# A state-space and spectral network on one core: the first layer's 68 slots written out, in place of a loop over pairs of them

## The chip, the cores and the metric

The kernel runs on one core of a Trainium2 chip. Its engines are PE (TensorE, matmuls, with its weight loads shown as PEld), DVE (VectorE), ACT (ScalarE), POOL (GpSimd) and SP (SyncE), which here only issues DMA transfers. Each runs its own instruction stream, and they wait for each other with semaphores. The metric is the device time of one execution, in microseconds.

## What is computed

The input is a batch of 4 images of 128 channels and 128 x 128 points, in float32. Two layers follow each other; the change is in the first. That one cuts each image into windows of 8 x 8 points and treats the 64 points of a window as a sequence:

```python
tn = (t - mu) * jax.lax.rsqrt(var + 1e-05) * ln_g + ln_b
xz = tn @ W_in + b_in                      # 256 inputs xi, 256 gates z
xc = sum((xp[:, k:k + L, :] * conv_w[:, k] for k in range(K))) + conv_b
xc = jax.nn.silu(xc)
dbl = xc @ W_x                             # rank 8 for delta, 16 rows of B, 16 of C
delta = jax.nn.softplus(dr @ dt_w + dt_b)
def step(h, inputs):
    dA = jnp.exp(d_t[:, :, None] * A)
    h = dA * h + (d_t * x_t)[:, :, None] * B_t[:, None, :]
    y = jnp.einsum('nds,ns->nd', h, C_t)
y = (ys.transpose(1, 0, 2) + xc * D) * jax.nn.silu(z)
out = y @ W_out + b_out                    # and + x
```

The second layer normalises over channels, filters in the frequency domain with 16 complex filters mixed by `Theta`, and ends in a two-matmul MLP with gelu.

## The kernel before

The program has four parts, each a block of five instruction streams: `setup`, `layer0` (the first layer), `spectral` and `mlp` (the second). The first layer works on 64 blocks of 1,024 tokens: a block is 8 rows of one image, 16 windows. It is done in halves of 512 tokens, for 16 states each, so a block has 32 **steps**; a step is one state of one half. In a step DVE scans (L919, `state`), PE or POOL makes what drives the scan (PE transposes `drive_r` at L591 from ACT's `ub`; POOL multiplies `drive_d` at L1034 from a row of B that SP has loaded as `b_all`), ACT makes the decay (L734), DVE or POOL multiplies the state with C (L930 with a row that PE spread into a PSUM bank at L582, L1045 with `c_all` loaded by SP), and PE adds the product into `y_acc` (L604). Between the steps lie the other jobs of the layer: mean and variance, the matmuls of `xz` and the convolution (L641, L646), `rows` and `c_rows` (L754, L755 on ACT, L945 on DVE), delta, the gate, the output and the first transform of the next layer.

The work is pipelined over blocks in **slots**. In slot m the 32 steps are those of block m; at fixed places among them stand the jobs that prepare blocks m + 1 and m + 2 and finish blocks m - 1 and m - 2. The order on every engine is written out by hand, in tables (`JOBS`, `AT`) that give each job its half step. With 64 blocks there are 68 slots, m = -2 to 65; in the first and last four some of the work is missing. Buffers alternate with the parity of m.

`slots` calls each engine's `body` for the slots in order. It writes out the first four, runs the 60 slots m = 2 to 61 as a loop of 30 passes, an even and an odd slot in each, and writes out the last four. In the loop the slot's number depends on the register `j`, and so does the value of every wait: `need` then waits for a value that register arithmetic (L182 as the recorded line) has computed. The loop is a construct of each engine's own stream: at its end stand an addition, a compare and a branch back (L167). DVE also computes, once a slot, the means and variances of eight rows in eight short instructions at L980; this document uses them as a clock mark of a slot.

Of the kernel before, what the change touches and what calls it, by code (L numbers as in the profile page):

```python
# [158 lines left out]

def slots(eng, body, blocks):  # L160
    rounds = (0, 0)
    for m in range(-2, 2):
        slot = Slot(m, True, m >= -1, m >= 0, m >= 1, False, rounds)
        body(slot, m % 2)
        rounds = tuple(r + k for r, k in zip(rounds, slot.size))
    per = tuple(sum(j[3] == bank for j in JOBS) for bank in range(2))
    with eng.Fori(0, (blocks - 4) // 2) as j:  # L167
        for i in range(2):
            body(Slot(j * 2 + 2 + i, True, True, True, True, True,
                      tuple(j * (2 * k) + (r + k * i) for r, k in zip(rounds, per))), i)  # L170
    rounds = tuple(r + k * (blocks - 4) for r, k in zip(rounds, per))
    for m in range(blocks - 2, blocks + 2):
        slot = Slot(m, False, m < blocks - 1, m < blocks, m <= blocks, True, rounds)
        body(slot, m % 2)
        rounds = tuple(r + k for r, k in zip(rounds, slot.size))

# [237 lines left out]
def layer0(nc, a, wt, rows_dram, x1_dram, y_dram, blocks):  # L414
    with ExitStack() as ctx:
# [87 lines left out]
        def _(sp):  # L503
# [65 lines left out]
            sp.sem_inc(s["x1_stored"], 16)  # L569
            sp.sem_inc(s["yo_stored"], 16)  # L570
            slots(sp, body, blocks)
            sp.wait_ge(s["x1_stored"], 16 * blocks + 16)
            sp.wait_ge(s["yo_stored"], 16 * blocks + 16)

        @block.tensor
        def _(pe):
# [129 lines left out]
            def body(S, p):  # L706
                for n in range(NSTEP):
# [9 lines left out]
                    jobs(S, p, 2 * n + 1)  # L717

            slots(pe, body, blocks)

        @block.scalar
        def _(act):
# [179 lines left out]

            act.preload_act_table_set(TABLES)
            slots(act, body, blocks)

        @block.vector
# [718 lines left out]
```

## Time and profile before

| | |
|---|---|
| median of 3 runs | 9539.61 us (9535.7 to 9547.48) |
| the profiled execution | 9544.83 us |
| its span, first to last instruction | 9543.0 us |
| mean granted TensorE clock | 0.986 |
| instructions recorded | 181,899 |
| PE, POOL, DVE, ACT busy, share of the span | 91%, 84%, 87%, 81% |
| DMA packets of the two queues that carry program code | 391 and 357 |

The span is what the trace covers, 1.8 us less than the execution's time. The first layer fills it from the beginning to about 6840 us, the spectral part to about 8990, the MLP the rest. A granted clock of 1 is TensorE at 2.4 GHz, of 0.5 at 1.2 GHz. An idle time put down to "issue" is one in which the engine waited for nothing that the trace shows.

### The profile page before, as it was taken

What the parts mean: (1) busy time and instruction counts of PE and PEld (TensorE: products, weight loads), DVE (VectorE), ACT (ScalarE), POOL (GpSimd) and SP (SyncE); (2) the same over time, 40 slices, a digit from 0 to 9 for tenths busy, and PEclk for the clock granted to TensorE, in tenths of its full rate; (3) what the DMA queues carried; (4) which work ended last, traced back from release to release, by engine and by line L of the source; (5) the groups of instructions that cost most, each with busy time, mean ns of one, the idle gap of its engine ahead of it and who ended that gap; (6) DMA issues with size and microseconds to landing.
All of it is one profiled execution on the core that took longest, in us unless ns stands there. A gap on an engine that the chain in (4) does not pass through costs nothing. (4 is left out here: it accounts for less than half of the span.)

```text
span 9543.0 us, 181899 instructions
## 1 busy us (share of the span) xinstructions
PE 8679.4 (91%) x54525; PEld 6752.8 (71%) x54525; DVE 8330.0 (87%) x8144; ACT 7711.4 (81%) x13926; POOL 8059.3 (84%) x3865
## 2 busy tenths in 40 slices
PE   7998999999899999989999999999799999999899
PEld 4666666666666666666666666666688888888788
DVE  5998999999889999998999999899788888888766
ACT  6998999999899999999999999999555555555577
POOL 5999999999999999999999999999688888888500
PEclk9999999999999999999999999999899999999999
DMA  3333333333333333333333333333200100010255
GB/s 90 113 115 113 109 117 109 113 110 119 109 108 114 115 114 108 117 112 110 110 119 113 110 116 109 114 108 120 76 32 31 36 31 32 31 36 31 78 185 178
DMA packets 648652, 933.96 MB, mean 98 GB/s; under 512 B 79961, under 2 KB 277601, under 8 KB 643553
## 3 DMA queue, kind: packets, MB, share of 16 engines
q1 hardware_dynamic: 647904, 924.64, 31.0%
q8 instruction: 391, 6.41, 0.3%
q14 instruction: 357, 2.92, 0.1%
HBM read 778.38 MB, written 146.04 MB: 97 GB/s over the span
## 5 line engine op out<-in xcount | busy, mean ns | idle before, releaser
L1045 POOL TENSOR_TENSOR prod<-state,c_all 128x1024 f32<-128x1024 f32 x1280 | 3028.2, 2370 | 176.8 <-DVE state L919 167.9
L919 DVE TENSOR_TENSOR_SCAN state<-decay_d,drive_d 128x1024 f32<-128x1024 f32 x1024 | 2337.2, 2282 | 158.0 <-issue 86.0
L1034 POOL TENSOR_TENSOR drive_d<-du,b_all 128x1024 f32<-128x1024 f32 x1024 | 2422.9, 2366 | 53.0 <-DMA b_all<-bc_rows 48.9
L919 DVE TENSOR_TENSOR_SCAN state<-decay_r,drive_r 128x1024 f32<-128x1024 f32 x1024 | 2325.0, 2271 | 28.4 <-PE drive_r L591 26.1
L604 PEld LDWEIGHTS y_acc<-ident,prod 128*128 128x128 f32 x16384 | 1861.5, 141 | 627.8 <-issue 532.5
L604 PE MATMUL y_acc<-ident,prod 128*128 128x128 f32 x16384 | 2152.3, 275 | 40.6 <-POOL prod L1045 36.8
L1342 DVE SCALAR_TENSOR_TENSOR sum_d<-bank_d,filt,sum_d 128x512 f32<-128x512 f32 x2470 | 1679.6, 744 | 268.2 <-PE bank_d L1250 241.3
L1389 POOL TENSOR_TENSOR sum_p<-sum_p,scaled 128x1024 f32<-128x1024 f32 x650 | 1551.7, 2387 | 261.5 <-ACT scaled L1300 229.5
L747 ACT ACTIVATE ub<-ut,bt 128x256 f32<-128x256 f32 x4096 | 1739.0, 499 | 16.1 <-PE drive_r L591 16.1
L1300 ACT ACTIVATE scaled<-bank_p,filt 128x512 f32<-128x512 f32 x1560 | 944.1, 688 | 734.5 <-PE bank_p L1250 660.0
L734 ACT ACTIVATE decay_d<-delta,neg_a 128x504 f32<-128x504 f32 x2048 | 1312.0, 674 | 64.0 <-DVE state L919 63.2
L734 ACT ACTIVATE decay_r<-delta,neg_a 128x504 f32<-128x504 f32 x2048 | 1344.0, 706 | 0.0
L591 PE MATMUL drive_r<-ident,ub 128*128 128x128 f32 x8192 | 1100.4, 278 | 234.6 <-issue 115.1
L591 PEld LDWEIGHTS drive_r<-ident,ub 128*128 128x128 f32 x8192 | 945.4, 143 | 456.5 <-issue 402.1
L930 DVE TENSOR_TENSOR prod<-state,job_bank 128x1024 f32<-128x1024 f32 x768 | 925.4, 1205 | 112.9 <-PE job_bank L582 107.1
L641 PE MATMUL job_bank<-x_in,tap_w 128*128 128x512 f32 (+3 forms) x2048 | 966.0, 594 | 3.7 <-DVE c_rows L945 2.4
L1250 PE MATMUL bank_d<-th_high,x_high 128*128 128x256 f32 x2600 | 792.5, 305 | 6.3 <-DVE x_low L1352 2.5
L1250 PE MATMUL bank_d<-th_low,x_high 128*128 128x256 f32 x2600 | 734.9, 283 | 0.0
L1250 PE MATMUL bank_d<-th_high,x_low 128*128 128x256 f32 x2600 | 734.8, 283 | 0.0
L641 PEld LDWEIGHTS job_bank<-x_in,tap_w 128*128 128x128 f32 x2048 | 353.6, 190 | 319.0 <-issue 301.8
L1052 POOL TENSOR_TENSOR delta<-delta,soft 128x512 f32<-128x512 f32 x256 | 326.8, 1277 | 288.6 <-ACT soft L791 288.6
L1250 PE MATMUL bank_p<-th_high,x_high 128*128 128x256 f32 x1560 | 474.2, 304 | 57.1 <-ACT scaled L1300 57.1
(155 smaller groups left out, 14712.8 us busy)
## 6 DMA issues: line engine op xcount, KB each, us to landing
c_all<-bc_rows SPq DMA_DIRECT2D x1280, 256.0 KB, 3.3
b_all<-bc_rows SPq DMA_DIRECT2D x1024, 256.0 KB, 3.8
ys<-row_spectra SPq DMA_DIRECT2D x130, 256.0 KB, 2.8
column_sums<-tt SPq DMA_DIRECT2D x130, 256.0 KB, 2.2
x_in<-in_x_dram SPq DMA_DIRECT2D x64, 512.0 KB, 4.5
x_res<-in_x_dram SPq DMA_DIRECT2D x64, 512.0 KB, 4.6
x_rows<-x SPq DMA_DIRECT2D x64, 512.0 KB, 4.5
row_spectra<-z SPq DMA_DIRECT2D x64, 512.0 KB, 3.7
```

Source lines behind the costliest of these rows:

```text
L591: mm = pe.matmul(drive_r[:, hf, g * P:(g + 1) * P], ub[place_of(RSTEPS, n, NS_UB)][:, g, hf * P:(hf + 1) * P], wt["ident"][:], start=True, ...
L604: mm = pe.matmul(y_acc[:, g, hf * P:(hf + 1) * P], prod[n % NP][:, hf, g * P:(g + 1) * P], wt["ident"][:], start=(n % NS == 0 and hf == 0 ...
L641: mm = pe.matmul(o[:, :, k:WT], wt["tap_w"][:, K - 1 - k, hf * P:(hf + 1) * P], v[:, :, 0:WT - k], start=(k == 0), stop=(k == K - 1), skip ...
L734: last = act.activation(dst[:, hf, :, 1:WT], delta[:, hf, q * HT:(q + 1) * HT].rearrange("p (w t) -> p w t", t=WT)[:, :, 1:WT], ACT.Exp, s ...
L747: last = act.activation(ub[place_of(RSTEPS, n, NS_UB)][:, g, :], ut[q][:, g, :], ACT.Copy, scale=bt[q][:, g, st:st + 1])
L919: dve.tensor_tensor_scan(state[n % NT][:].rearrange("p h t -> p (h t)"), decay[:].rearrange("p h w t -> p (h w t)"), drive[:].rearrange("p ...
L1034: pool.tensor_tensor(drive_d[place_of(DSTEPS, n, ND)][:], du[:, :, q * HT:(q + 1) * HT], b_all[slot][:].unsqueeze(1).to_broadcast([P, 2, HT]),
L1045: pool.tensor_tensor(prod[n % NP][:], state[n % NT][:], c_all[slot][:].unsqueeze(1).to_broadcast([P, 2, HT]), ALU.mult).then_inc(s["prod_g ...
L1250: mm = pe.matmul(o, x[p][:, part, b, :], th[:, 2 * pair:2 * pair + 2, :].rearrange("p l h -> p (l h)"), start=(b % 2 == 0 and i == 0), sto ...
L1300: act.activation(scaled[n % 2][:, i, out, :].rearrange("p (b h) -> p b h", b=B), bank_p[:, :, i, :], ACT.Copy, scale=filt[p][:, kind, 2 * ...
L1342: dve.scalar_tensor_tensor(acc, src, factor, acc, ALU.mult, ALU.add).then_inc(s["summed_d"], 1)
L1389: pool.tensor_tensor(acc, acc, scaled[n % 2][:, i], ALU.add).then_inc(s["summed_p"], 1)
```

## The change

`slots` loses the loop. All 68 slots are written out, with m as a plain number; the flags of what a slot contains follow from m. Every value waited for is then a constant. What each engine computes, in which order, and which semaphores it waits for, stay the same.

```diff
 def slots(eng, body, blocks):
     rounds = (0, 0)
-    for m in range(-2, 2):
-        slot = Slot(m, True, m >= -1, m >= 0, m >= 1, False, rounds)
-        body(slot, m % 2)
-        rounds = tuple(r + k for r, k in zip(rounds, slot.size))
-    per = tuple(sum(j[3] == bank for j in JOBS) for bank in range(2))
-    with eng.Fori(0, (blocks - 4) // 2) as j:
-        for i in range(2):
-            body(Slot(j * 2 + 2 + i, True, True, True, True, True,
-                      tuple(j * (2 * k) + (r + k * i) for r, k in zip(rounds, per))), i)
-    rounds = tuple(r + k * (blocks - 4) for r, k in zip(rounds, per))
-    for m in range(blocks - 2, blocks + 2):
-        slot = Slot(m, False, m < blocks - 1, m < blocks, m <= blocks, True, rounds)
+    for m in range(-2, blocks + 2):
+        slot = Slot(m, m < blocks - 2, -1 <= m < blocks - 1, 0 <= m < blocks, 1 <= m <= blocks, m >= 2, rounds)
         body(slot, m % 2)
         rounds = tuple(r + k for r, k in zip(rounds, slot.size))
```

In the built program the first layer's loop bodies hold 1299 entries on PE (a matmul and its weight load counted once), 611 on ACT, 398 on DVE, 278 on POOL and 188 on SP. Written out, the first layer has 36,604 on PE, 14,649 on ACT, 7,875 on DVE, 5,822 on POOL and 2,948 on SP; before it had 3,585, 1,522, 895, 642 and 378.

The place that matters is where an odd slot ends and an even one begins. On DVE this is, before the change, the end of the loop body: the last steps of the odd slot, register arithmetic between them, and the branch.

```order
L182 REGISTER_ALU
L919 SCALAR_TENSOR_TENSOR state2<-decay_d,drive_d3 128x1024
L182 REGISTER_ALU
L919 SCALAR_TENSOR_TENSOR state3<-decay_r1,drive_r 128x1024
L182 REGISTER_ALU x2
L930 TENSOR_TENSOR prod2<-state2,job_bank0 128x1024
L167 REGISTER_ALU
L167 COMPARE_AND_BRANCH
```

The branch leads back to the start of the body, where the register values of the pass are made and the even slot begins:

```order
L167 ISA
L182 ISA
L919 SCALAR_TENSOR_TENSOR state0<-decay_d,drive_d0 128x1024
L182 ISA
L919 SCALAR_TENSOR_TENSOR state1<-decay_r0,drive_r 128x1024
L182 ISA x2
L945 TENSOR_TENSOR c_rows1<-job_bank1,c_rows1 16x512
```

After the change the same place of DVE's stream, between slot 3 and slot 4 (the line numbers are ten lower, L909 for L919):

```order
L920 TENSOR_TENSOR prod0<-state0,job_bank0 128x1024
L909 SCALAR_TENSOR_TENSOR state2<-decay_d,drive_d3 128x1024
L909 SCALAR_TENSOR_TENSOR state3<-decay_r1,drive_r 128x1024
L920 TENSOR_TENSOR prod2<-state2,job_bank0 128x1024
L909 SCALAR_TENSOR_TENSOR state0<-decay_d,drive_d0 128x1024
L909 SCALAR_TENSOR_TENSOR state1<-decay_r0,drive_r 128x1024
L935 TENSOR_TENSOR c_rows1<-job_bank1,c_rows1 16x512
L920 TENSOR_TENSOR prod0<-state0,job_bank0 128x1024
```

The arithmetic and the branch are gone, and nothing that computes has moved.

## Rows read from the trace of the kernel before

**Rows 1.** The page: busy time of each engine, share of the span, instructions.

```profile
PE 8679.4 (91%) x54525; PEld 6752.8 (71%) x54525; DVE 8330.0 (87%) x8144; ACT 7711.4 (81%) x13926; POOL 8059.3 (84%) x3865
```

**Rows 2.** Table of stretches: us, busy per engine, PEclk, DMA share, GB/s.

```profile
3029.50:3036.00 6.50, 2.47 (x19) 1.92 (x17) 3.92 (x3) 2.83 (x5) 5.16 (x4) 1.00 0.96 262
3036.00:3040.00 4.00, 3.83 (x12) 2.56 (x13) 3.81 (x2) 0.27 (x1) 4.00 (x3) 0.57 0.25 91
3134.50:3236.80 102.30, 94.64 (x586) 69.29 (x585) 95.47 (x75) 96.61 (x180) 96.78 (x49) 1.00 0.37 115
```

**Rows 3.** Timeline of DVE at L980: start us, us, operation.

```profile
381.40 0.63 DVE L980 BATCH_NORM_AGGREGATE mv<-stats 128x2 f32<-128x6 f32 x8
...
484.78 0.63 DVE L980 BATCH_NORM_AGGREGATE mv<-stats 128x2 f32<-128x6 f32 x8
...
3001.69 0.64 DVE L980 BATCH_NORM_AGGREGATE mv<-stats 128x2 f32<-128x6 f32 x8
...
3108.98 0.64 DVE L980 BATCH_NORM_AGGREGATE mv<-stats 128x2 f32<-128x6 f32 x8
...
3211.30 0.64 DVE L980 BATCH_NORM_AGGREGATE mv<-stats 128x2 f32<-128x6 f32 x8
...
6565.12 0.63 DVE L980 BATCH_NORM_AGGREGATE mv<-stats 128x2 f32<-128x6 f32 x8
```

**Rows 4.** Timeline at one turn; in brackets the idle time before, and releaser.

```profile
3031.36 0.61 PE L612 MATMUL y_acc<-diag_d,xc 128*128 128x128 f32 x4
...
3032.23 1.20 DVE L930 TENSOR_TENSOR prod<-state,job_bank 128x1024 f32<-128x1024 f32 x1
...
3035.68 2.35 POOL L1034 TENSOR_TENSOR drive_d<-du,b_all 128x1024 f32<-128x1024 f32 x1 [1.34 <-DMA b_all<-bc_rows]
...
3036.17 1.96 PE L591 MATMUL drive_r<-ident,ub 128*128 128x128 f32 x8 [4.20 <-issue]
3036.19 2.29 DVE L919 TENSOR_TENSOR_SCAN state<-decay_d,drive_d 128x1024 f32<-128x1024 f32 x1 [2.77 <-issue]
...
3039.73 0.69 ACT L770 ACTIVATE zs<-job_bank,z_b 128x512 f32<-128x512 f32 x1 [7.03 <-PE job_bank L646]
...
3043.01 0.68 DVE L945 TENSOR_TENSOR c_rows<-job_bank,c_rows 16x512 fp32r<-16x512 f32 x1 [2.35 <-ACT c_rows L755]
```

**Rows 5.** Table of waits, 600 to 6590 us: us, times, longest.

```profile
PE drive_r L591 <- issue: 111.4, 28, 5.0
...
DVE state L919 <- issue: 83.0, 28, 4.0
...
DVE c_rows L945 <- ACT c_rows L755: 58.8, 26, 3.2
```

**Rows 6.** DMA queues, 600 to 6590 and 3029.5 to 3039.5 us: packets, MB, share.

```profile
q8 instruction: 342, 5.60, 0.4%
q14 instruction: 312, 2.56, 0.1%
...
q1 hardware_dynamic: 1714, 2.00, 70.4%
q8 instruction: 2, 0.03, 1.2%
q14 instruction: 4, 0.03, 1.0%
```

**Rows 7.** Timeline of DVE, and table of stretches, at a slow interval.

```profile
1221.01 0.64 DVE L980 BATCH_NORM_AGGREGATE mv<-stats 128x2 f32<-128x6 f32 x8
...
1324.40 0.64 DVE L980 BATCH_NORM_AGGREGATE mv<-stats 128x2 f32<-128x6 f32 x8
...
1234.00:1239.00 5.00, 5.00 (x27) 4.47 (x28) 4.29 (x4) 3.59 (x8) 5.00 (x3) 0.68 0.14 41
```

**Rows 8.** Timeline of DVE: last scans of slots 61 and 62.

```profile
6593.48 2.26 DVE L919 TENSOR_TENSOR_SCAN state<-decay_r,drive_r 128x1024 f32<-128x1024 f32 x1
...
6695.32 2.26 DVE L919 TENSOR_TENSOR_SCAN state<-decay_r,drive_r 128x1024 f32<-128x1024 f32 x1
```

## The prediction

> **What bounds the kernel now.** I read the page first: no engine is saturated over the span, the busiest four lie between 81% and 91% [rows 1]. So the busy time says little about this change; the question is what paces a slot of the first layer. The table of stretches answers it for 102.3 us, one slot long, that hold no turn of the loop: POOL is busy 96.78, ACT 96.61, DVE 95.47 and PE 94.64 [rows 2]. Nothing is idle for more than 8%; the slot is a braid of short waits between four nearly full engines, and whatever delays one of them by microseconds is not absorbed.
>
> Next, the timeline at one operation that DVE does once in a slot (the eight aggregations of L980). Inside a loop pass, from the even slot to the odd one, it advances from 3108.98 to 3211.30, 102.3 us; from the odd slot to the next even one, across the loop's turn, from 3001.69 to 3108.98, 107.3 us [rows 3]. Every other slot is longer by 5.
>
> The timeline around one turn shows where the 5 us lie [rows 4]. PE's last matmuls of the pass start at 3031.36, its first of the next pass only at 3036.17, after 4.20 us in which it waited for nothing the trace names ("issue"). DVE ends a product at 3033.43 (3032.23 + 1.20) and starts the next scan at 3036.19, 2.77 us of "issue". ACT then stands for 7.03 us until 3039.73, held by the late PE; and because ACT is late, DVE loses another 2.35 us at 3043.01. POOL is the exception: it goes on at 3035.68 and what it waited for was the row of B. The table of waits says that this is the rule: 28 such idle times of DVE of 83.0 us in all, 28 of PE of 111.4, and 26 waits of DVE for ACT's c_rows of 58.8, in a stretch that holds 28 turns [rows 5]. In the same microseconds the DMA engines are busiest (0.96 of their share against 0.37 in the slot without a turn), and just behind it PE's granted clock is 0.57, so part of that stretch runs at 1.2 instead of 2.4 GHz [rows 2].
>
> I read this as program code that is not there when the jump lands: PE, DVE and ACT each have a loop body too long to keep and must bring its start in again, POOL's shorter one is kept. The trace shows code as two queues of its own, 342 and 312 packets in 5990 us, about 23 in a loop pass of 209.7 us; six of them fall in the ten microseconds after PE ran dry, where the data queue holds 70% of the DMA engines [rows 6].
>
> **The change, part by part.**
>
> *Turns removed.* The loop makes 30 passes, so 29 turns; all go. From the aggregation at 484.78 (slot 3) to that at 6565.12 (slot 61) there are 58 intervals, 29 across a turn and 29 inside a pass: 6080.34 us [rows 3]. Inside a pass most intervals are 102.30; four of the 29 are 103.4 to 103.5, as from 1221.01 to 1324.40, where PE's granted clock falls to 0.68 for some microseconds late in the slot [rows 7]. Their mean is (25 x 102.30 + 4 x 103.46) / 29 = 102.46. Without turns all 58 would take between 58 x 102.30 = 5933.4 and 58 x 102.46 = 5942.7, a gain of 146.9 or 137.6. I take 102.40, between them, since the same weak place stays in every slot and only its timing against the clock's grants is open: 5939.2, a gain of **141 us**. The waits give the same from the other side: 29 x (83.0 / 28 + 58.8 / 26) = 152 [rows 5], a little too much, since DVE waits some tenths for c_rows in turn-free slots too. One turn is worth 6080.34 / 29 - 2 x 102.40 = 4.9.
>
> *Is a slot of written-out code as fast as one in the loop?* The old kernel has both. Its last scans of slots 61 and 62 start at 6593.48 and 6695.32 [rows 8]: 101.84 across the loop's end and through written-out code with constant waits (slot 62 lacks the work for later blocks, so it should not be longer). No cost of leaving the loop, and no sign that constants speed up a slot. At the other end, slot 2 to 3, the loop's first pass, takes 103.38 (381.40 to 484.78) [rows 3]. This is my bound on the bad side: if all 58 kept 103.38, they would take 5996.0 and the gain would be 84.
>
> *Register arithmetic removed.* In a pass each engine computes the numbers it waits for; in the built program that is 165 entries of DVE's 398, 219 of PE's 1299. Some come back as pure waits, because two waits now share one entry but a compute instruction holds few (DVE 84 to about 98 in a pair of slots, PE 59 to about 124). They lie beside running instructions: DVE reads ahead while a 2.3 us scan runs. I price this at nothing; what hides it is the length of the compute instructions. Were a tenth of a microsecond saved at six hand-overs of each slot, it would be 58 x 0.6 = 35 us more; the row into slot 62 speaks against it. The other way, more pure waits on PE could cost as much, and the same row speaks against that.
>
> *Code brought in.* A pair of slots needs its code once, where the loop needed it once too and at the turn a part again. SP and POOL, which kept their bodies, must now stream theirs. All of it is read in order, as the middle of each pass is today: of about 23 packets in a pass six lie at the turn, the other 17 arrive in running code, and DVE's scans show 28 "issue" waits for 28 turns and none beyond [rows 5, 6]. Price: nothing in time; the cover is reading ahead, and without it a late block costs what a turn costs, 4.9.
>
> *What a page says.* The Trainium skill, "Runtime: NRT & Kernel Launch", section on instruction fetch mechanics, holds that reading ahead is sequential and a taken branch to code outside the held window must wait for a fetch; rows 4 agree for PE and DVE. "Advanced Engine Details and Errata", section on control flow timing, prices a compare-and-branch at about 108 ns. By that alone 29 turns would be worth an estimated 3 us and the kernel would stay at about 9537; the 2.77 us in front of DVE's scan is against it.
>
> *The later layers* keep their loops and code; I change nothing there. They only lie at other addresses.
>
> **Sum.** The profiled run took 9544.8 us around a span of 9543.0 and stands 5.2 above the median of 9539.6. 9544.8 - 141 = 9403.8; against the median **9399 us**.
>
> **Rivals.**
>
> *Clock and fill pace.* Without a turn to shift them, slots may meet the half-clock spell [rows 7] in most passes, 1.1 us each, that is at the pace of slot 2 to 3: gain 84, about 9456. For it: both are in the trace. Against: 25 of 29 turn-free intervals escape it. 10%.
>
> *Straight code also stalls.* This is the one that ends slower. Place: DVE or PE in mid-slot, when a transfer of 512 KB fills the queues just as a block of code is due (the share of 0.96 in rows 2). Price 4.9 us for each late block. It decides from one late block in each pair of slots, which cancels the gain; with two it is 9540 + 29 x 4.9 = 9682. Against it: 17 packets in each pass arrive today without a stall. For it: SP and POOL have hardly streamed code so far, and SP issues every load of B and C. 3% for slower, 3% for cancelling out.
>
> *The branch is not the cause*, the 5 us belong to the slot's own end (the DMA burst, slot edges) and stay: 9540. Against it: the edge inside a pass has the same work and shows 102.3. 2%.
>
> *Constants pay too*: 20 to 35 us more, 9365 to 9380. 7%.
>
> **How the numbers follow.** The main case, gain 120 to 150, gets 75%; 9399 lies in it. The range 9370 to 9436 holds it, most of the constants' case and the milder half of the clock case (half the slots with a spell), and leaves out less than 2 in 10. What can be told from no change is about 0.2%, 19 us: faster 0.92, same 0.05, slower 0.03 (the main, the clock and the constants' case are faster, the branch's and the cancelling one the same).
>
> **What the new profile would show.** Aggregations of L980 (ten lines higher) 102.3 to 102.5 apart throughout, none at 107. No "issue" wait of DVE's scan and PE's drive_r transposes; DVE's waits for c_rows below 10 us in all. The first layer's last y copy about 141 us earlier, the two later layers as long as before. Code queues with 530 to 600 packets instead of 748 on the page, and some 162,000 records instead of 181,899. Wrong would be: intervals of 102.3 broken by "issue" waits of 3 us or more at places fixed in the code (streaming stalls), a granted clock below 0.98 in the layer (clock case), or regular intervals near 104.7 (not the branch).

## The result, and the profile after

| | before | after |
|---|---|---|
| median | 9537.66 us (9531.39 to 9547.48, 4 runs) | 9406.23 us (9402.15 to 9408.65, 4 runs) |
| ratio | | 0.9861, interval 0.9844 to 0.9878 |
| profiled execution | 9544.83 us | 9405.45 us |
| mean granted TensorE clock | 0.986 | 0.991 |
| packets of the two code queues | 391 and 357 | 321 and 256 |

The change gained 131.4 us between the medians and 139.4 us between the two profiled executions; the forecast was 9399, seven below what was measured. First the head of the page, beside [rows 1]:

```profile
span 9403.6 us, 162094 instructions
...
PE 8642.4 (92%) x54525; PEld 6728.5 (72%) x54525; DVE 8324.0 (89%) x8144; ACT 7708.3 (82%) x13926; POOL 8054.7 (86%) x3865
```

The engines do the same work (POOL 8054.7 us against 8059.3, DVE 8324.0 against 8330.0) in a shorter span. PE's busy time is 37 us less; its matmuls are the same, the granted clock is 0.991 instead of 0.986. Between slots 3 and 61 the clock stood at its lower level (1.2 GHz) for 150 us before and for 38 after, 30 spells against 11; 26 of the 30 lay behind a turn, which has 29. Next the clock mark of a slot, DVE's eight aggregations, ten lines higher than in [rows 3] (start us, us, operation):

```profile
486.46 0.64 DVE L970 BATCH_NORM_AGGREGATE mv<-stats 128x2 f32<-128x6 f32 x8
588.62 0.64 DVE L970 BATCH_NORM_AGGREGATE mv<-stats 128x2 f32<-128x6 f32 x8
...
895.11 0.64 DVE L970 BATCH_NORM_AGGREGATE mv<-stats 128x2 f32<-128x6 f32 x8
998.48 0.63 DVE L970 BATCH_NORM_AGGREGATE mv<-stats 128x2 f32<-128x6 f32 x8
...
6425.20 0.63 DVE L970 BATCH_NORM_AGGREGATE mv<-stats 128x2 f32<-128x6 f32 x8
```

From slot 3 to slot 61 it is 5938.7 us, before it was 6080.3: 141.6 less. No interval is 107 any more. Apart from a pair of 102.5 and 101.8 between slots 29 and 31 and one of 102.35, they are either 102.16, as from 486.46 to 588.62, or 103.37, as from 895.11 to 998.48; the long one comes 11 times in the 58, nearly always every fifth slot. The table of stretches shows one of either kind, then a piece of the long one, then the place where the turn was (columns as in [rows 2]):

```profile
3046.50:3148.66 102.16, 94.62 (x587) 69.28 (x585) 95.36 (x76) 96.59 (x180) 96.66 (x49) 1.00 0.36 115
2943.12:3046.50 103.38, 95.70 (x587) 70.97 (x585) 95.61 (x75) 96.70 (x180) 96.82 (x49) 0.98 0.37 114
2955.50:2960.50 5.00, 4.54 (x21) 3.99 (x21) 4.89 (x5) 3.60 (x7) 5.00 (x4) 0.66 0.26 100
2972.00:2978.00 6.00, 4.76 (x26) 3.14 (x26) 6.00 (x4) 3.56 (x7) 5.53 (x4) 1.00 0.98 285
```

The long slot holds the stretch with a clock of 0.66 over 5 us, which is 3.4 us at 1.2 instead of 2.4 GHz. In the last row the DMA engines are as full as at the turn before (0.98), yet DVE is busy for all of the 6 us. The timeline of that place, the start of slot 28, answers to [rows 4] line by line:

```profile
2975.13 1.09 PE L581 MATMUL drive_r<-ident,ub 128*128 128x128 f32 x8 [1.18 <-DVE state L909]
2976.11 2.28 DVE L909 TENSOR_TENSOR_SCAN state<-decay_d,drive_d 128x1024 f32<-128x1024 f32 x1
2976.46 2.35 POOL L1024 TENSOR_TENSOR drive_d<-du,b_all 128x1024 f32<-128x1024 f32 x1 [0.47 <-issue]
...
2977.43 0.69 ACT L760 ACTIVATE zs<-job_bank,z_b 128x512 f32<-128x512 f32 x1 [1.87 <-PE job_bank L636]
...
2980.77 0.68 DVE L935 TENSOR_TENSOR c_rows<-job_bank,c_rows 16x512 fp32r<-16x512 f32 x1 [0.20 <-ACT c_rows L745]
```

PE's 4.20 us of "issue" are a wait of 1.18 for DVE's scan, DVE's 2.77 are nothing, ACT's 7.03 are 1.87, and DVE's 2.35 before c_rows are 0.20. The table of waits, 600 to 6450 us, which holds 57 slots (us in total, times, longest; beside [rows 5]):

```profile
DVE prod L920 <- issue: 82.8, 57, 1.8
...
PE drive_r L581 <- DVE state L909: 74.2, 172, 1.2
...
DVE c_rows L935 <- ACT c_rows L745: 11.5, 57, 0.2
DVE state L909 <- issue: 8.3, 11, 0.8
```

The first row looks like the "late block of code in mid-slot" that the prediction called wrong for it, though its longest wait is 1.8 us and the prediction spoke of 3 or more. It is next to no new idle time. The kernel before has this row for the same product, 600 to 6590 us, also 57 slots:

```profile
DVE prod L930 <- PE job_bank L582: 99.6, 114, 1.5
```

There the product waited twice a slot, and the trace named PE's c row as what it waited for. After the change 82.8 us are put down to "issue", 18.1 to DVE's own scan and 3.1 to PE's row, 104.0 together. A run below, with register values in the waits, shows the old name again at the same speed. My reading, which no run tests by itself, is that two waits share one entry in the constant form and that the label follows the other.

Over the same stretch the code queues carried less, beside the first two of [rows 6]:

```profile
q8 instruction: 275, 4.51, 0.3%
q14 instruction: 218, 1.79, 0.1%
```

### The profile page after: what moved, and what is told of

The parts are those of the page before. It is cut to its first block and busy times, and to the rows that moved or that the text cites. A ratio compares the mean times of both kernels' runs of the same rounds, so it can differ in the third digit from the quotient of the medians.

```text
span 9403.6 us, 162094 instructions
## 1 busy us (share of the span) xinstructions
PE 8642.4 (92%) x54525; PEld 6728.5 (72%) x54525; DVE 8324.0 (89%) x8144; ACT 7708.3 (82%) x13926; POOL 8054.7 (86%) x3865
## 5 line engine op out<-in xcount | busy, mean ns | idle before, releaser
L909 DVE TENSOR_TENSOR_SCAN state<-decay_d,drive_d 128x1024 f32<-128x1024 f32 x1024 | 2336.3, 2282 | 76.5 <-ACT decay_d L724 76.4
L909 DVE TENSOR_TENSOR_SCAN state<-decay_r,drive_r 128x1024 f32<-128x1024 f32 x1024 | 2322.7, 2268 | 27.4 <-PE drive_r L581 16.3
L581 PE MATMUL drive_r<-ident,ub 128*128 128x128 f32 x8192 | 1078.4, 275 | 101.0 <-DVE state L909 93.2
```

What stands on the lines that cost most here:

```text
L581: mm = pe.matmul(drive_r[:, hf, g * P:(g + 1) * P], ub[place_of(RSTEPS, n, NS_UB)][:, g, hf * P:(hf + 1) * P], wt["ident"][:], start=True, ...
L909: dve.tensor_tensor_scan(state[n % NT][:].rearrange("p h t -> p (h t)"), decay[:].rearrange("p h w t -> p (h w t)"), drive[:].rearrange("p ...
```

## The experiments

Each is the kernel after with the edit shown, except where the kernel before is named. Written-out kernels repeat to within a few microseconds: in the kernel after and four variants without a turn on PE, DVE or ACT the medians lie between 9402 and 9408.

### Four slots in a pass

```diff
-    for m in range(-2, blocks + 2):
...
+    with eng.Fori(0, (blocks - 4) // 4) as j:
+        for i in range(4):
+            body(Slot(j * 4 + 2 + i, True, True, True, True, True,
+                      tuple(j * (4 * k) + (r + k * i) for r, k in zip(rounds, per))), i % 2)
```

> The loop again, but with four slots in a pass: 15 passes and 14 turns in place of 29. Theory (each turn costs 4.9 us because PE, DVE and ACT must bring in the code at its target, and nothing else in the loop costs): 9406 + 14 x 4.9 = 9475, intervals of L980 of about 107 once in four slots and near 102.3 otherwise. Rival (the register arithmetic and register waits of the loop cost, turn or no turn): as the old kernel, 9538. Rival (a longer body is dearer to bring in): above 9500.

Measured: 9461.91 us (9457.15 to 9468.94), 55.7 above the kernel after, with 14 turns in place of 29: 4.0 for each, where 4.9 were expected (9475). Its marks, across a turn and the interval behind it, and its waits, 600 to 6500 us:

```profile
690.83 0.64 DVE L980 BATCH_NORM_AGGREGATE mv<-stats 128x2 f32<-128x6 f32 x8
798.68 0.63 DVE L980 BATCH_NORM_AGGREGATE mv<-stats 128x2 f32<-128x6 f32 x8
900.98 0.63 DVE L980 BATCH_NORM_AGGREGATE mv<-stats 128x2 f32<-128x6 f32 x8
...
PE drive_r L591 <- issue: 45.0, 14, 4.1
DVE state L919 <- issue: 38.8, 14, 3.4
```

The time follows the number of turns, and so do the "issue" waits: 14 of each. The interval right behind a turn is 102.30, the two after it 102.13. So the 102.30 that the prediction took for the undisturbed slot still had an echo of the turn in it.

### A loop of a single pass, and one of two

```diff
-    with eng.Fori(0, (blocks - 4) // 4) as j:
-        for i in range(4):
+    with eng.Fori(0, 1) as j:
+        for i in range(blocks - 4):
```

> The 60 middle slots stand in a loop that makes a single pass: no turn, but every value waited for is still made by register arithmetic. Theory (turns cost, arithmetic nearly nothing): 9406 plus at most 58 x 0.14 = 8 us, since a turn-free interval was 102.30 in the old kernel and is 102.16 in the new one: 9406 to 9414. Rival (constants are what made it faster): 9538.

Measured: 9405.33 us (9401.97 to 9407.26). It doesn't test what it was built for. Its trace records 162,109 instructions, 15 more than that of the kernel after, where the old loop has 181,899: with a single pass the program was built with constants. It is a second measurement of the kernel after, no more. The question was asked again with two passes of 30 slots, which has register values in all waits of the middle slots and one turn:

```diff
-    with eng.Fori(0, (blocks - 4) // 4) as j:
-        for i in range(4):
+    with eng.Fori(0, 2) as j:
+        for i in range(30):
```

> The first layer's 60 middle slots as a loop of two passes of 30 slots on every engine: every wait is made by register arithmetic again, but there is one turn only, from slot 31 to 32. (The loop of a single pass tried before had been folded back: it records the same number of arithmetic instructions as the kernel without a loop, so its waits were constants.) Theory, turns are all and register arithmetic is free: the intervals between the aggregations of L980 are 102.1 to 102.2 with some at 103.4, as in the kernel after; one interval, at the turn, is 3 to 6 us longer; 9406 + 5 = 9411, range 9403 to 9416. Rival, constants in the waits pay: a tenth of a microsecond at six hand-overs of each slot is 0.6 us a slot, the intervals are 102.5 or more and the time 9430 to 9450.

Measured: 9402.97 us (9401.95 to 9407.53), at the lower edge of what was expected, with 181,339 instructions. Its marks around the one turn, and its waits, 600 to 6450 us:

```profile
3352.14 0.63 DVE L980 BATCH_NORM_AGGREGATE mv<-stats 128x2 f32<-128x6 f32 x8
3457.17 0.64 DVE L980 BATCH_NORM_AGGREGATE mv<-stats 128x2 f32<-128x6 f32 x8
3559.49 0.63 DVE L980 BATCH_NORM_AGGREGATE mv<-stats 128x2 f32<-128x6 f32 x8
...
DVE prod L930 <- PE job_bank L582: 94.8, 114, 1.5
...
POOL prod L1045 <- issue: 2.3, 1, 2.3
DVE state L919 <- issue: 2.2, 1, 2.2
PE drive_r L591 <- issue: 2.2, 1, 2.2
```

One interval is 105.03, the next 102.32, all others 102.15, 102.3 or 103.3. The turn cost 3.1 us once, and 19,000 more instructions of register arithmetic cost nothing that can be measured: this kernel isn't slower than the one written out in full. The constants' case is out.

### One engine's loop at a time

In each of these only the named engines keep the old loop over pairs of slots, and the others are written out (`slots_loop` is the old function):

```diff
-            slots(pe, body, blocks)
+            slots_loop(pe, body, blocks)
```

PE alone:

> Only PE keeps the loop over two slots; the other four engines have their 68 slots written out. Theory: PE's idle time of some 4.2 us at its turn returns, and through it ACT's late z and DVE's late c_rows; since both DVE's own stall and PE's ended at the same c_rows in the old trace, nearly the whole price returns: 9525 to 9545. Rival (the price is mainly DVE's own stall of 2.9 us): 9406 + 29 x 2 = 9464 or less. Rival (register arithmetic on PE): no issue wait of 4 us at the turn, but slower everywhere.

DVE alone:

> Only DVE keeps the loop over two slots. Theory: at its turn DVE reads ahead about 3 us before it runs dry, and its code takes 4 to 5.5 us to come; so at most 2 us per turn are lost, and fewer when the fetch no longer shares the queue with PE's and ACT's: 9406 + 29 x (1 to 2) = 9435 to 9465. Rival (prices of the engines add up to the whole, so that PE's 79 us leaves 42 for DVE and ACT together): DVE and ACT each 10 to 30, so 9416 to 9436. Rival (the engine does not matter): 9485 as with PE.

ACT alone:

> Only ACT keeps the loop over two slots. Theory: ACT has two decays (2 x 0.67 twice, 2.7 us) in hand when it passes the branch, then stands until its code is there after 4 to 5.5 us, and in the written-out kernel it waits 1.7 us for PE's z matmul at that place anyway: some 0 to 1.5 us a turn, 9406 to 9450. Rival (prices add up): 9416 to 9436. Rival (the engine does not matter): 9485.

POOL and SP:

> Only POOL and SP keep the loop; PE, DVE and ACT are written out. Theory (their bodies, 278 and 188 instructions, stay in reach and a turn takes 0.3 us): no cost, 9403 to 9410. Rival (every turn costs, whatever the body's length): POOL is as busy as DVE, so 9450 to 9540.

| loops on | median (range) | above the kernel after |
|---|---|---|
| PE | 9485.06 (9464.70 to 9497.78) | 78.8 |
| DVE | 9527.82 (9522.64 to 9537.11) | 121.6 |
| ACT | 9427.26 (9425.23 to 9429.87) | 21.0 |
| POOL and SP | 9403.89 (9402.83 to 9407.25) | -2.3 |

For PE and for DVE the expectation missed, in opposite directions: I had taken PE for nearly the whole of the price, and it is DVE that alone brings back most of it. The three prices sum to 221, the whole is 131: they overlap. The waits of the kernel with PE's loop, 600 to 6500 us:

```profile
DVE c_rows L953 <- ACT c_rows L763: 60.9, 57, 3.1
PE drive_r L599 <- issue: 37.5, 19, 3.5
```

And with DVE's loop:

```profile
DVE state L927 <- issue: 72.6, 28, 3.5
PE job_bank L649 <- DVE c_rows L953: 72.5, 28, 3.5
```

With PE late, ACT and then DVE's c_rows are late (60.9 us, against 11.5 where nothing turns). With DVE late, c_rows is late by itself and PE stands for it, 28 times, 72.5 us. The timeline of one of these turns, with what PE and DVE do in it:

```profile
3036.63 2.29 DVE L927 TENSOR_TENSOR_SCAN state<-decay_d,drive_d 128x1024 f32<-128x1024 f32 x1 [2.62 <-issue]
...
3041.13 0.68 DVE L953 TENSOR_TENSOR c_rows<-job_bank,c_rows 16x512 fp32r<-16x512 f32 x1
...
3041.87 3.38 PE L649 MATMUL job_bank<-x_in,tap_w 128*128 128x512 f32 x4 [2.62 <-DVE c_rows L953]
...
3046.31 2.29 DVE L927 TENSOR_TENSOR_SCAN state<-decay_r,drive_r 128x1024 f32<-128x1024 f32 x1 [1.05 <-PE drive_r L599]
```

DVE comes back 2.62 us late. c_rows is its third instruction from there; PE stands 2.62 us for it and then needs 3.38 us for four matmuls that take 1.97 at the same place in the kernel after, because its granted clock has fallen (mean of 3036 to 3044 us: 0.83). That makes `drive_r` late, and DVE waits another 1.05. Its own 2.6 us became 4.1 in the mean interval (106.46 against 102.39). The mean clock of this run is 0.984, the kernel after has 0.991.

What the clock adds can be read in this same run, since its turns differ in it. Three intervals across a turn (columns as in [rows 2]), and DVE's first scan behind the second and the third turn; that of the first stands above:

```profile
3002.16:3108.23 106.07, 95.90 (x587) 69.87 (x586) 95.57 (x76) 96.95 (x180) 97.01 (x49) 0.98 0.37 112
3210.49:3318.20 107.71, 97.45 (x587) 71.11 (x586) 95.56 (x75) 96.95 (x180) 97.17 (x49) 0.97 0.35 110
4255.56:4360.23 104.67, 94.45 (x587) 69.29 (x586) 95.46 (x76) 96.96 (x180) 96.75 (x49) 1.00 0.36 114
...
3245.03 2.29 DVE L927 TENSOR_TENSOR_SCAN state<-decay_d,drive_d 128x1024 f32<-128x1024 f32 x1 [2.69 <-issue]
4290.04 2.29 DVE L927 TENSOR_TENSOR_SCAN state<-decay_d,drive_d 128x1024 f32<-128x1024 f32 x1 [2.62 <-issue]
```

DVE stands for 2.62, 2.69 and 2.62 us. Where the clock stayed up, the interval is 104.67; with a spell of half clock, beginning while PE stands for c_rows, it is 106.07, and with a spell twice as long 107.71. So a spell adds 1.4 or 3.0 us to a stall of the same length. It came at 27 of DVE's 29 turns (8 of them the long kind), at 13 of PE's 29 and at one of ACT's. At 1.4 and 3.0 us each, an estimate of the clock's share is 51 us of DVE's 122 and 25 of PE's 79: the larger part of what lies between the two. With PE alone looping, the 16 turns without a spell have intervals of 103.1 to 104.0 us and the 13 with one 105.2 to 108.4. There the first code packet of the first queue started 1.1 to 1.7 us after the branch at 17 turns, one of which had a spell, and 3.0 to 4.3 us after it at 12, all of which had one: the later the code, the longer PE stands, and behind the long stands the clock is down.

The code queues tell whose code came twice: with PE's loop the first queue has 391 packets instead of 321 and the second its 256; with DVE's loop they are 321 and 346, with ACT's 321 and 327. POOL and SP in a loop give 321 and 195: they bring in less than written out, since they keep their bodies. It saves no time, as streaming costs none.

### The store at the turn

The 512 KB store of the first transform fills the DMA engines at the turn. In the kernel before I moved its issue four steps on in SP's order (26 to 30). That hardly moves the store itself, which waits for the data it stores: it leaves 27.5 us behind the slot's mark instead of 26.5. But the loads of B and C that stood behind it in SP's order now go ahead of it. At the turn of [rows 4] six of them left within 3.4 us after the store; in the same slot here it is one:

> The old kernel with its loop; only the store of 512 KB at the end of a slot (row_spectra) is issued four steps later, so that five loads of B and C no longer pile up behind it and leave with it just before the turn. Theory (the code of the turn waits behind that burst: with PE alone looping, its first code packet started 1.2 to 1.6 us after the branch in half of the turns and 3.4 to 4.2 in the others, and PE went on after 3.8 to 4.2 or 5.5 to 6.9): PE goes on about 4 us after its branch instead of 6.2, 29 x 2.2 = 64 us less than the old kernel, 9440 to 9480. Rival (the time to bring in code is its own and has nothing to do with the data): no change, 9510 to 9540.

Measured: 9487.47 us (8 runs, 9478.87 to 9517.46), ratio to before 0.9960 (0.9943 to 0.9977): 47 us below the 9534.32 of the kernel before beside it, and seven above what was expected. The burst in front of the turn is thus over a third of the price (47 of 128 us). From its branch to its first register entry of the next pass PE took 5.4 us (median; 6.2 in the kernel before), DVE 4.8 (5.6). PE was expected to need about 4. So in the next pair the store goes out in two halves, at step 27 and at step 2 of the next slot, and in the looped one the loop also starts a slot later, so that its turns lie at the other parity. The lines are from `AT` and from SP's stream:

```diff
-    "x_in": 15, "rows": (17, 0), "rows_landed": (24, 6), "x1_out": 16, "x_res": 25, "yo_out": 26,
+    "x_in": 15, "rows": (17, 0), "rows_landed": (24, 6), "x1_out": 16, "x_res": 25, "yo_out": (27, 2),
...
+            def store_yo(at, half):
+                rows = slice(4 * half, 4 * half + 4)
```

> The loop over two slots again on all engines (28 turns, it now begins with slot 3), but the store of 512 KB at the end of a slot is cut in two: the first half goes four steps earlier than the turn, the second two steps behind it, so that neither it nor the loads that piled up behind it stand in front of the code. Output unchanged. Theory (code waits in the queues behind data): PE goes on 3.5 to 4.2 us after its branch instead of 6.2, DVE after 3 to 3.5 instead of 5.5, and with 2.8 us of work in hand DVE loses under 1 us itself; a turn costs 1 to 2.5 us, 9434 to 9476. Rival (bringing in code takes 5 us of its own, burst or not): 9487 or more, as with the store only four steps later.

> The changed kernel with the same store in two halves. Theory (with no turn nothing waits for the burst but a few rows of B, 10.6 us of POOL's idle time in all): 9396 to 9407. Rival (the burst costs in its own right, and part of what the loop lost was the burst): 9380 or less.

Measured: in the loop, with 28 turns, 9483.34 us (9473.02 to 9489.82); written out, 9407.71 (9406.49 to 9408.75), 0.7 above its expected range, where the kernel after has 9406.23. The waits of the looped one, 600 to 6500 us:

```profile
PE drive_r L602 <- issue: 61.0, 24, 2.9
DVE c_rows L956 <- ACT c_rows L766: 42.7, 26, 2.3
DVE state L930 <- issue: 25.4, 19, 1.6
```

The intervals across its turns are 105.05 in the mean, 2.75 above the others; the old kernel's were 4.75 above. So more than half of the price is there without the full store. From branch to the next pass PE still took 4.8 us, DVE 3.7 and ACT 3.8. In written-out code the store costs nothing in either form (9407.71 with halves, 9406.23 whole). The looped kernel missed its expectation (at most 9476) by seven: I had given the burst more of the price than it has. How much is the store's and how much the turn's other place, this pair doesn't separate. The place did change something: POOL, whose next pass began 0.27 us after its branch in the kernel before, took 2.6 us here, and the second code queue has 493 packets where the kernel before has 357. At the turn behind slot 28 POOL had work for 3.6 us in hand and did not stand, so this delay cost nothing there.

### The spectral loop written out too

```diff
-            with eng.Fori(1, (KY - 1) // 2) as j:
+            for j in range(1, (KY - 1) // 2):
```

SP's own loop, a few lines on, is written out in the same way.

> The changed kernel, and the loop of the spectral part (31 passes of 65.5 us) written out too. Theory (its bodies, at most 175 instructions on DVE and 97 on ACT, stay in reach, and PE's does too): its turns cost next to nothing, 9400 to 9408. Rival (every turn costs 2.7 to 5 us): 30 x 3 to 5 = 9256 to 9316.

Measured: 9402.08 us (9400.64 to 9402.24), ratio to before 0.9870. It is the lowest of all, by 4 us against the kernel after and by 1 against the two-pass loop: within what separates two measurements of the written-out kernel. The spectral part's turns cost at most these few microseconds.

### Filling the place where the clock falls

The slow slots have their spell of half clock just behind the variance matmuls, for which PE waits (1.09 us for ACT's square in the slot shown above). Six matmuls with no use, identity by identity, were put in front of each. The wait, in that slot:

```profile
2954.01 1.10 PE L623 MATMUL job_bank<-sq,mean_w 128*128 128x512 f32 x2 [1.09 <-ACT sq L792]
```

The edit:

```diff
                 elif kind == "var":
                     q = int(name[-1])
+                    for _ in range(6):
+                        pe.matmul(misc[:, 0:P], wt["ident"][:], wt["ident"][:], start=True, stop=True)
```

> The changed kernel; before each of the two variance matmuls, where PE stands about 1.1 us for ACT's squares, PE does six more matmuls of 128 columns on constants (results overwritten, output unchanged). In the changed kernel one slot in five takes 103.4 instead of 102.16, each time with the granted clock at its half level at the same step 25. Theory (that spell comes from PE's idle time ahead of it): the 12 slow slots vanish, 12 x 1.2 = 15 us less: 9388 to 9396. Rival (the spell has nothing to do with PE's idle time): 9406, slots still 103.4 one in five. Rival (the added matmuls delay the variance and cost): above 9410.

Measured: 9478.17 us (9473.75 to 9481.33), 72 slower; missed, on the side of the last rival. Two groups of its table by line, 600 to 6450 us (busy, mean ns | idle before):

```profile
L922 DVE TENSOR_TENSOR prod<-state,job_bank 128x1024 f32<-128x1024 f32 x680 | 820.3, 1206 | 172.2 <-issue 147.9 <-DVE state L911 18.1 <-PE job_bank L572 0.3
...
L623 PE MATMUL job_bank<-ident 128*128 128x128 f32 x1368 | 176.0, 278 | 0.0
```

The fill takes 3.1 us of PE in each slot, and DVE's product now waits twice a slot for a row that PE spreads (147.9 us of "issue" in 114 waits, it was 82.8 in 57). An interval is 103.5, where 102.16 was; the 65 us more of DVE's waits are 1.1 of the 1.35 in each slot. PE has no 3 us to give at this place: the fill delays what stands behind it. Fewer slots have the half-clock spell (8 between slots 3 and 61, where 11 had it), so it did move the clock; but the 1.35 us that it costs in each slot are more than the 1.2 that a spell costs in one of five.

## Why the prediction was right

**The sum.** The prediction put the 58 intervals at 5939.2 us; they took 5938.7. The gain in this stretch was to be 141, it is 141.6; slot 3 is reached 1.7 us later than before and the rest of the program takes 0.5 more, which leaves the 139.4 between the two spans. The first DMA issue of the spectral part lies at 6687.05, before it was 6827.72.

**The mean slot.** 102.40 was a choice between 102.30 and 102.46, and it held because two errors partly cancelled and I had stood between the bounds. The undisturbed slot is 102.15, not 102.30, since the old in-pass interval carried an echo of the turn: 58 x 0.15 = 8.7 us better. And 11 of 58 slots meet the half-clock spell, where 4 of 29 did: 3 more than the proportion, 3.6 us worse. From the upper bound, 5942.7 - 8.7 + 3.6 = 5937.6, a microsecond from the 5938.7 measured. That is the mild end of the clock rival; at its full size (every slot 103.38) it did not come. The interval from slot 2 to 3, from which that bound was taken, says nothing about loop or written-out code: it is 103.38 before and 103.39 after, with a spell of half clock in both (granted clock 0.86 over 388 to 400 us before, 0.76 over 394 to 401 after).

**The step that failed: from the profiled run to the median.** I took the old profiled run's 5.2 us above its median off the new time as well: 9404 became 9399. But the old kernel's runs differ by their turns. Its times are 9503 to 9556 us over all the runs beside these experiments, and its intervals across a turn reach from 103.8 to 109.1 in one profile, while all runs of the kernel after lie within 7 us. Only one old execution has a trace, so this is inferred and not shown, but what makes one of them longer than another seems to be what the change removes. Then nothing was to be taken off; 9404 is 2 from the 9406.23 measured.

**What a turn is.** That it is code which must be brought in at the branch was read from idle time and from packets; the runs bear it out. The time falls with the number of turns (29, 14, 1: 131, 56 and nothing measurable above the kernel after), the "issue" waits count them, and each of the long loops alone adds packets to one of the two code queues. The page "Runtime: NRT & Kernel Launch" of the Trainium skill, section on instruction fetch mechanics, says that a taken branch out of the held window stalls until its target is fetched; the two-pass loop, in which POOL waits at the turn with the others, agrees with 2.2 to 2.3 us in front of each. The page "Advanced Engine Details and Errata" of the Trainium skill, section on control flow timing, gives about 108 ns for a compare-and-branch, and by that alone 29 turns would have been worth an estimated 3 us; they were worth 131.

**The clock's part of it.** The prediction saw the clock of 0.57 behind the turn, but took the turn's price as one sum and spoke of the clock only for slots without a turn. Three intervals across a turn of the kernel before (columns as in [rows 2]) tell the two apart:

```profile
1324.40:1429.66 105.26, 94.37 (x587) 69.30 (x586) 95.47 (x76) 96.64 (x180) 96.97 (x50) 1.00 0.34 112
2162.04:2268.50 106.46, 95.77 (x586) 70.10 (x585) 95.47 (x75) 96.62 (x180) 96.99 (x49) 0.98 0.35 112
3211.30:3319.09 107.79, 96.84 (x587) 70.70 (x586) 95.48 (x75) 96.75 (x180) 97.17 (x49) 0.97 0.36 110
```

PE's idle time at these turns is 3.71, 3.57 and 3.84 us and DVE's 3.10, 2.97 and 3.12, nearly the same. The clock makes the difference: up throughout, down for a spell, down for one twice as long; 1.2 and 2.5 us more. Of the 29 turns 12 have the shorter spell and 14 the longer. An estimate from these rows is 12 x 1.2 + 14 x 2.5 = 49 us, over a third of the 138 by which the 29 intervals were longer. The rest is the stall for code itself.

**Who pays for it.** The prediction took the 2.35 us before c_rows as the price of PE being late, and ACT's 7.03 too. With PE's loop alone that holds (60.9 us before c_rows). But it doesn't follow that PE bears the price: alone, PE's turns cost 79 us, DVE's 122, ACT's 21. It didn't matter for the sum, because all went together; an edit of PE's stream alone would have been mispriced.

**Register arithmetic, streaming, later layers.** Priced at nothing, and each stood up: two passes with all the arithmetic 9402.97; POOL and SP streaming or not, 9403.89 against 9406.23; nothing moved behind the layer. Of the lesser forecasts, 577 code packets lie in 530 to 600, DVE's waits for c_rows are 11.5 us where I had said below 10, and 8.3 us of "issue" before the scan remain.

**What stays open.** Why the half-clock spell comes in nearly every fifth slot; why it comes behind some turns and not behind others with the same stall; and how the price of a turn divides between the burst of data, of which 47 us are shown, and the place of the branch.

## What to carry to other kernels

An idle time put down to "issue", once for each turn of a loop and on each engine with a long body, is a cost of the turn and goes with the number of turns: a loop of a few long passes gives all of the gain (two passes of 30 slots: 9402.97 us) without the whole program written out. In a braid of nearly full engines the price of one engine's stall is not its own idle time (72.6 us for DVE) but the time with all that follows from it (122 us): the others stand, and in 27 of DVE's 29 turns TensorE's clock fell too. Prices of single engines don't add up. And where the old time varies because of what is removed, compare the new time with the profiled run itself, not with the median moved by a difference.

## What the hardware showed that I had not expected

- A turn has no fixed price. In one profile of the kernel before, intervals across it run from 103.8 to 109.1 us; with only PE looping most are either 103.1 to 103.5 or 106 to 108.4. What divides them is whether TensorE's granted clock fell behind the turn: with the same 2.62 us of idle time on DVE an interval is 104.67 with the clock up and 106.07 with a spell of half clock.
- POOL's body of 278 entries was kept from pass to pass in the old kernel. In the two-pass loop it is not (2.3 us of "issue"). Length is not all: a loop over two slots that began one slot later did not keep POOL's either (2.6 us from branch to next pass, against 0.27).
- In the written-out kernel the clock's half-level spell settles into a pattern: nearly every fifth slot, at the same place, 1.2 us each. In the old kernel four of 29 slots without a turn had it.
